# First half of a conv attention kernel: partitions (y half, x), Sx by column tiles without masks, Yh in quarter-array tiles over two banks

## The reference

```python
qkv = einsum('bcxy,oc->boxy', img, w_qkv)            # q, k, v of 512 channels each
k = softmax(k over the 4096 pixels)
content_out = einsum('nde,ndm->nem', einsum('ndm,nem->nde', k, v), q)
Sx = einsum('ndxy,xid->nixy', q4, Px)                # Px[x,i] = rel_rows[i-x+63]
Yh = einsum('nixy,neiy->nexy', Sx, v4)               # then batch norm over all n, x, y
Sy = einsum('ndxy,yid->nixy', q4, Py)                # Py from rel_columns, the same way
rel_pos_out = einsum('nixy,nexi->nexy', Sy, Yh)
out = einsum('bcxy,oc->boxy', content_out + rel_pos_out, w_out) + b_out
```

## Time and profile before

| | |
|---|---|
| median of three runs | 3277.91 us |
| the profiled execution's own time | 3290.07 us |
| its span, first to last instruction | 3288.2 us |
| mean granted TensorE clock | 0.932 of 2.4 GHz |
| PE busy (matmul) | 2756.5 us, 84% |
| DVE busy | 2293.0 us, 70% |
| ACT busy | 1874.7 us, 57% |
| POOL busy | 1111.6 us, 34% |
| first half | from 0 to about 1982 us |

### The profile page before, as it was taken

How to read it: one execution, slowest core, us unless ns; L and a number is a source line. 1 busy time by engine, 2 the same in 40 slices (tenths; PEclk the granted TensorE clock), 3 DMA queues, 4 the chain that set the end, 5 groups by cost and what they waited for, 6 DMA issues and landing times. The chain is left out here.

```text
span 3288.2 us, 102882 instructions
## 1 busy us (share of the span) xinstructions
PE 2756.5 (84%) x42610; PEld 2189.8 (67%) x42610; DVE 2293.0 (70%) x3437; ACT 1874.7 (57%) x3268; POOL 1111.6 (34%) x495
## 2 busy tenths in 40 slices
PE   2898998998997988988989981787978787888888
PEld 2687787776876877777778771656565655665655
DVE  5687787786786876787786665756575656665665
ACT  2575665756666666575575652546464545555553
POOL 1223313224133133142241316553434334352530
PEclk9999999999999999999999995898989898989989
DMA  3133323323324224234232336766766757676663
GB/s 131 44 88 112 87 65 118 92 60 118 86 66 131 67 71 139 60 77 127 66 92 56 79 92 130 149 183 145 185 145 172 159 167 171 161 170 160 160 162 105
DMA packets 419610, 381.99 MB, mean 116 GB/s; under 512 B 296784, under 2 KB 363600, under 8 KB 413008
## 3 DMA queue, kind: packets, MB, share of 16 engines
q1 hardware_dynamic: 399632, 341.13, 41.9%
q10 hardware_dynamic: 19520, 34.15, 2.9%
HBM read 206.37 MB, written 168.82 MB: 114 GB/s over the span
## 5 line engine op out<-in xcount | busy, mean ns | idle before, releaser
L365 PE MATMUL bank<-w_hi,x_hi 128*128 128x256 f16 x2048 | 577.9, 282 | 46.6 <-POOL x_lo L700 23.4
L365 PE MATMUL bank<-w_lo,x_hi 128*128 128x256 f16 x2048 | 570.7, 279 | 0.0
L365 PE MATMUL bank<-w_hi,x_lo 128*128 128x256 f16 x2048 | 570.3, 278 | 0.0
L715 POOL TENSOR_TENSOR k_f<-k_f,negmax 128x1024 f32<-128x1024 f32 x64 | 181.6, 2859 | 940.7 <-DVE negmax L675 940.7
L1153 POOL TENSOR_TENSOR y_f<-y_f,y_mul 128x1024 f32<-128x1024 f32 x126 | 264.6, 2100 | 662.9 <-DMA y_f<-y_scratch 661.6
L1096 DVE TENSOR_TENSOR yb_lo<-y_f,yb_hi 64x1024 f16<-64x1024 f32 x256 | 381.7, 1491 | 80.8 <-ACT yb_hi L996 79.1
L652 DVE SCALAR_TENSOR_TENSOR sx_lo<-bank,parity,sx_hi 128x512 f16<-128x512 f32 x512 | 355.2, 743 | 51.7 <-ACT sx_hi L490 51.1
L942 PE MATMUL bank<-q,rc_both 128*64 128x64 f16 x4096 | 282.9, 245 | 97.9 <-issue 47.0
L480 ACT ACTIVATE k_f<-bank 128x256 f32<-128x256 f32 x512 | 198.8, 388 | 244.2 <-PE bank L365 233.8
L490 ACT ACTIVATE sx_hi<-bank,parity 128x512 f16<-128x512 f32 x512 | 321.2, 703 | 26.1 <-PE bank L365 18.4
L942 PEld LDWEIGHTS bank<-q,rc_both 128*64 128x64 f16 x4096 | 252.4, 134 | 125.0 <-issue 76.4
(11 more groups left out here) (149 smaller groups left out, 9009.0 us busy)
## 6 DMA issues: line engine op xcount, KB each, us to landing
y_scratch<-yst SPq DMA_DIRECT2D x512, 128.0 KB, 2.0
y_f<-y_scratch SPq DMA_DIRECT2D x64, 1024.0 KB, 11.9
q<-q_scratch SPq DMA_DIRECT2D x256, 256.0 KB, 11.9
x_f<-x SPq DMA_DIRECT2D x16, 2048.0 KB, 10.9
q_scratch<-q_hi SPq DMA_DIRECT2D x64, 512.0 KB, 5.8
q_scratch<-q_lo SPq DMA_DIRECT2D x64, 512.0 KB, 7.4
x_res<-x SPq DMA_DIRECT2D x128, 256.0 KB, 4.3
out<-x_res ACTq DMA_DIRECT2D x128, 256.0 KB, 3.3
```

The source lines that it names most:

```text
L365: mm = pe.matmul(outs, lhs[a], rhs[m], start=first and n == 0, stop=last and n == 2, **kw)
L715: pool.tensor_tensor(kk, kk, negmax[:, :].unsqueeze(1).to_broadcast([P, 8, P]), ALU.add).then_inc(shifted_b, 1)
```

## The change

- Partitions: `x_hi`/`x_lo` are kept as (y half, x, y) instead of (x, y half, y). The kv weights then give v and k with partitions (g, x) instead of (x, g); the bytes read per matmul and their strides stay.
- sx: the table holds the two halves one after the other (`g*P`), and each step issues 48 matmuls of 64 weights x 64 columns, two column tiles (g = 0, 1) side by side, instead of 24 of 128 weights. The output partitions are (g, i), the order of v's, so Sx is kept once, without masks: one ACT copy and one DVE subtraction for a step.
- yh: for each y, a tile of 64 rows x 64 weights for each (g, head), 64 columns; g = 0 goes to one bank and g = 1 to the next, so two steps are made together: 96 matmuls for two steps (48 a step instead of 24). PE waits until both banks are free. Both `filled` counts come with the last matmuls of the 96.
- Order in stretch A: q 0, q 1, yh 0, yh 1, q 2, q 3, yh 2, yh 3, ... The chain's pieces stay at the same counts j.
- A yh step holds 8 values of y of one half, and its store is one DMA of twice the size.

```diff
-                if not (first and hp == 0):
-                    order.append(("yh", hp - 1, i))
+                if i % 2 == 1 and not (first and hp == 0):
+                    order += [("yh", hp - 1, i - 1), ("yh", hp - 1, i)]
...
-                    dve.tensor_copy(rr_f[s, g:2 * NREL:2], rel_in[s, 0, :]).then_inc(s_zero, 1)
+                    dve.tensor_copy(rr_f[s, g * P:g * P + NREL], rel_in[s, 0, :]).then_inc(s_zero, 1)
...
-            x_hi = sb("x_hi", [P, CC, PIX], F16, p1)
+            x_hi = sb("x_hi", [P, CC, 2, H, HALF], F16, p1)
...
-                    for g in range(2):
-                        sp.dma_start(y_dram[b * HP + hp, g, 4 * i:4 * i + 4].rearrange("y h e x -> (h e) y x"),
-                                     yst[:, i % YST, :, g, :]).then_inc(y_st[i % YST], 16)
+                    k, g = i // 2, i % 2
+                    sp.dma_start(y_dram[b * HP + hp, g, 8 * k:8 * k + 8].rearrange("y h e x -> (h e) y x"),
+                                 yst[:, i % YST, :, :]).then_inc(y_st[i % YST], 16)
...
                             for j in range(8):
                                 xx = 8 * i + j
-                                mm = pairs(bank[:, r, j * 64:j * 64 + 64],
-                                           [s[:, 2 * (H - 1 - xx):2 * (H - 1 - xx) + P] for s in (rr_hi, rr_lo)],
-                                           [s[:, :, xx // XB, :, xx % XB] for s in (q_hi, q_lo)], True, True)
-                        else:
+                                for k, (a, m) in enumerate(TERMS):
+                                    for g in range(2):
+                                        mm = pe.matmul(bank[g * 64:g * 64 + 64, r, j * 64:j * 64 + 64],
+                                                       (rr_hi, rr_lo)[a][:, g * P + H - 1 - xx:g * P + H - 1 - xx + 64],
+                                                       (q_hi, q_lo)[m][:, :, xx // XB, :, xx % XB],
+                                                       start=k == 0, stop=k == 2)
+                        elif i % 2 == 0:
...
-                            for j in range(4):
+
+                            pe.wait_ge(freed, N + 2)
+                            pe.sem_inc(yh_begun, 1)
+                            banks = (r, (r + 1) % BANKS)
+                            for j in range(8):
                                 y2 = 4 * i + j
                                 for k, (a, m) in enumerate(TERMS):
-                                    for h2 in range(2):
-                                        own = slice(h2 * 64, h2 * 64 + 64)
-                                        mm = pe.matmul(bank[own, r, j * 128:j * 128 + 128],
-                                                       (v_hi, v_lo)[a][:, hp % 2, y2, own],
-                                                       (sx_hi, sx_lo)[m][:, h2 * HALF + y2, :, :].rearrange("p g x -> p (g x)"),
-                                                       start=k == 0, stop=k == 2)
-                        mm.then_inc(filled, 1)
+                                    for g in range(2):
+                                        half = slice(g * 64, g * 64 + 64)
+                                        for h2 in range(2):
+                                            own = slice(h2 * 64, h2 * 64 + 64)
+                                            mm = pe.matmul(bank[own, banks[g], j * 64:j * 64 + 64],
+                                                           (v_hi, v_lo)[a][half, hp % 2, y2, own],
+                                                           (sx_hi, sx_lo)[m][half, h2 * HALF + y2, :],
+                                                           start=k == 0, stop=k == 2)
+                                        if j == 7 and k == 2 and g == 0:
+                                            mm.then_inc(filled, 1)
+                        if kind != "yh" or i % 2 == 0:
+                            mm.then_inc(filled, 1)
...
-                            for g in range(2):
-                                o = act.activation(sx_hi[:, :, g, 8 * i:8 * i + 8],
-                                                   src.rearrange("p (x h) -> p h x", x=8),
-                                                   ACT.Copy, scale=parity[:, g:g + 1])
-                            o.then_inc(hi_done, 1)
+                            act.activation(sx_hi[:, :, 8 * i:8 * i + 8], src.rearrange("p (x h) -> p h x", x=8),
+                                           ACT.Copy).then_inc(hi_done, 1)
...
-                                o = dve.scalar_tensor_tensor(sx_lo[:, :, g, s],
-                                                             src.rearrange("p (x h) -> p h x", x=8),
-                                                             parity[:, g:g + 1], sx_hi[:, :, g, s],
-                                                             ALU.mult, ALU.subtract)
-                            o.then_inc(freed, 1)
+                            dve.tensor_tensor(sx_lo[:, :, s], src.rearrange("p (x h) -> p h x", x=8), sx_hi[:, :, s],
+                                              ALU.subtract).then_inc(freed, 1)
```

More of the change, by code:

```diff
@@ L222, in attention_kernel @@
         with p1, nc.Block() as block:
[L223 to L224 removed]
+            x_hi = sb("x_hi", [P, CC, 2, H, HALF], F16, p1)
+            x_lo = sb("x_lo", [P, CC, 2, H, HALF], F16, p1)
             k_f = sb("k_f", [P, HALF, P], F32, p1)
@@ L232, in attention_kernel @@
             q_lo = sb("q_lo", [P, 2, H // XB, HALF, XB], F16, p1)
-            sx_hi = sb("sx_hi", [P, 2 * HALF, 2, H], F16, p1)
-            sx_lo = sb("sx_lo", [P, 2 * HALF, 2, H], F16, p1)
-            yst = sb("yst", [P, YST, 4, 2, H], F32, p1)
+            sx_hi = sb("sx_hi", [P, 2 * HALF, H], F16, p1)
+            sx_lo = sb("sx_lo", [P, 2 * HALF, H], F16, p1)
+            yst = sb("yst", [P, YST, 8, H], F32, p1)
             k_max = sb("k_max", [P, 8, P], F32, p1)
@@ L278, in attention_kernel @@
             y_stats = sem("y_stats", p1)
+            yh_begun = sem("yh_begun", p1)
             init = sem("init", p1)
@@ L282, in attention_kernel @@
             XC = PIX // NXC
+            XR = H // NXC
             NBN = 16 + 1 + 2 + 2 + 1 + 4 + 2
@@ L295, in chain, with x_piece @@
                 return [(h, j) for h, j in start if 0 <= j < 16]
+            def x_piece(c, j):
+                return x_f[:, c, j * XC:j * XC + XC].rearrange("p (x g y) -> p g x y", g=2, y=HALF)
             def turns(eng, turn):
@@ L302, in turns @@
                 turn(NB - 1, final_turn)
-            xh_kv = [t[:, :, :].rearrange("p c (k y) -> p c y k", y=HALF) for t in (x_hi, x_lo)]
-            xh_q = [t[:, :, :].rearrange("p c (x g y) -> p c g x y", g=2, y=HALF) for t in (x_hi, x_lo)]
+            xh_kv = [t[:, :, :, :, :].rearrange("p c g x y -> p c y (g x)") for t in (x_hi, x_lo)]
             w_kv = [t[:, :, HID:3 * HID].rearrange("p c (t n) -> p c t n", t=2) for t in (w_hi, w_lo)]
@@ L356, in _ @@
                 for s in range(YST):
-                    sp.wait_ge(y_st[s], 32 * (NT * YH // YST + 1))
+                    sp.wait_ge(y_st[s], 16 * (NT * YH // YST + 1))
                 sp.wait_ge(x_in, 16 * CC * NB)
@@ L458, in split_x @@
                     act.wait_ge(x_norm, nth * 8 + piece * CC + 1)
-                    s = slice(piece * XC, piece * XC + XC)
-                    act.activation(x_hi[:, 0, s], x_f[:, 0, s], ACT.Copy).then_inc(x_hi_a, 1)
+                    act.activation(x_hi[:, 0, :, piece * XR:piece * XR + XR, :], x_piece(0, piece),
+                                   ACT.Copy).then_inc(x_hi_a, 1)
                 for piece in range(NXC):
@@ L475, in turn @@
                         if kind == "yh":
-                            act.wait_ge(y_st[i % YST], (t * (YH // YST) + (i // YST + 1)) * 32)
+                            act.wait_ge(y_st[i % YST], (t * (YH // YST) + (i // YST + 1)) * 16)
                         act.wait_ge(filled, at(b, (kind, hp, i)) + 1)
@@ L593, in split_x @@
                 def split_x(nth, j):
-                    s = slice(j * XC, j * XC + XC)
+                    s = slice(j * XR, j * XR + XR)
                     dve.wait_ge(x_norm, nth * 8 + (CC * j + 2))
-                    dve.tensor_copy(x_hi[:, 1, s], x_f[:, 1, s]).then_inc(x_hi_b, 1)
+                    dve.tensor_copy(x_hi[:, 1, :, s, :], x_piece(1, j)).then_inc(x_hi_b, 1)
                     dve.wait_ge(x_hi_a, nth * NXC + (j + 1))
-                    dve.tensor_tensor(x_lo[:, 0, s], x_f[:, 0, s], x_hi[:, 0, s], ALU.subtract).then_inc(x_lo_done, 1)
+                    dve.tensor_tensor(x_lo[:, 0, :, s, :], x_piece(0, j), x_hi[:, 0, :, s, :],
+                                      ALU.subtract).then_inc(x_lo_done, 1)
                 for k in range(16):
@@ L649, in turn @@
                         elif kind == "sx":
-                            for g in range(2):
-                                s = slice(8 * i, 8 * i + 8)
-                                o = dve.scalar_tensor_tensor(sx_lo[:, :, g, s],
```

(12 more changed lines are left out.)

6 lines of the change are left out of this document (3 added, 3 removed).

## The result

The changed kernel took 3306.32 us (median of 9 runs, 3292.87 to 3312.53), the kernel before 3285.02 us (9 runs beside them). The ratio is 1.0053, with a 95% interval from 1.0031 to 1.0075: slower by half a per cent. The sign was right, the size was not: the time lies between the forecast and the faster rival (3212 us, chance 0.14), and well nearer to no change than to either.

A forecast was written before the change was run, and what follows sets the result against it. PE was taken to bound nearly everything. B +134 us, A 31 x 0.6, last head pairs -10, first -2, very last -2.5 gave +138: 3428 us from 3290.07, or 3416 as median; range 3355 to 3510.

The forecast's parts named there:

- The sign: Whole kernel: slower, chance 0.83; within 0.2% 0.03; faster 0.14.
- faster rival: sx on PE: short matmuls in tiles overlap fully, 30 ns a pair, -66 us, 3212 us; chance 0.14.
- sx on PE: Each sx step: 24 pairs of column tiles at Sy's 62 ns, 1.49 us a step, where 0.72 us before.
- B: Stretch of sx and kv in turn, 23 head pairs: 23.8 us, against 17.2, 17.7 and 19.2 before; cost 134 us.
- B and C of the last head pairs: Last head pair of an image, sx alone then kv: 14.5 us against 14.9, then 21.0 against 22.7.
- changes of tiling: PE switching between 128x128 and column tiles: 0.1 us, twice for each sx among kv.
- lower bound: sx pair on PE: 30 ns, 0.72 us a step, if a strided moving operand in tiles were no slower than the present sx.
- yh on PE: yh steps in stretch A: 12 groups of four quarter tiles a step, 0.72 us taken, where 0.67 us before.
- first rival: yh on PE: quarter tiles don't overlap beyond pairs, 31 ns a matmul, 1.49 us a step, 3500 us; chance 0.21.
- Stretch A by hand: Stretch of q and yh: 28.0 us against 27.4, +0.6, with PE waits of 2.8 and 1.1 us.
- Half clock: Stretch B: half speed costs 1.7 us before; after, sx is blind to it, so 1.3 us.
- DVE and ACT relief: sx pieces: about 0.65 us a step saved on each, some 170 us busy time each, worth something only in last head pairs' B.

The follow-up runs named there:

- sy_contig: Changed kernel with Sy in the second half reading q as 64 neighbouring elements instead of 32 pieces of two (wrong q values): ratio 0.9961 to the kernel before.
- late_phi: Changed kernel with the four copies to p_hi on ACT two steps later and p_lo on POOL one step later: ratio 0.9955 to the kernel before.
- yh_pairs: Changed kernel with yh one bank at a time, two quarter tiles side by side, order q, yh, q, yh: ratio 1.0051 to the kernel before.
- sx_whole: Changed kernel with sx as 24 full-array matmuls instead of 48 on column tiles, half of Sx wrong: ratio 0.9867 to the kernel before.
- sx_twos: Changed kernel with two sx steps in a row, then two kv steps, where they alternate: ratio 1.0024 to the kernel before.
- fill_after: Changed kernel with unread matmuls in PE's idle time, 20 ahead of yh 6 and 10 ahead of sx 0: ratio 0.9986 to the kernel before.

## Why the prediction was wrong, by its own steps

**sx on PE, "I take 24 x 62 = 1.49 us a step": this step failed.** It measured 0.77 us plus 0.03. I priced the pair by the row of the same weights, columns and tiles (Sy), and called the moving operand a reason only in the rival. sy_contig shows that the moving operand makes all of the difference. The inference behind it held for Sy (a rate that is the same at both clocks is not set by the columns) but did not carry over: the new sx does follow the clock (54 ns a pair at half clock, 33 at full), and so does Sy with the other operand. By the step: the period of sx and kv on PE is 2.36 us (0.77 + 0.13 + 1.26 + 0.20) where I had 3.0, so 0.64 x 8 x 23 = 118 us too much, against the 120 us by which the profiled execution missed the sum. That the two agree so well is luck. B itself is 19.9, 20.1 and 19.8 us where I had 23.8, 89 us less in all, because a longer half clock and waits took up the rest; A came out 44 us below its forecast in all, and B and C of the last head pairs 15 us above theirs.

The sign is in part luck too. The term that was to make the kernel slower, 0.77 us more for a step's pairs, was 0.08. What did make B longer are the changes of tiling, which the forecast had as a small term and rightly sized, and the half clock, which it let shrink.

The lower bound I gave, 30 ns by the present sx, was the row with the same moving operand, and it was nearly right. Its rival then failed at the other end: at a pair of 33 ns it said faster, because it set its sum of steps for B, 17.6 us, against the measured 17.2, and so had B "where it was" although it counted 0.2 us of changes in each step, and took the half clock for 1.3 us. B is 2.2 us longer by the steps alone (7 x 0.30 + 0.08): 0.19 us of changes, 0.08 of pace, 0.03 in the kv behind. So its turning point, 36 ns, was too high; nor does it follow from the rival's own sums, where -66 us at 30 ns and 4.4 us for each ns of the pair (24 x 8 x 23 pairs) give 45 ns.

The sum had a slip besides: the 0.6 us of A stand in the 31 head pairs and again in the seven last head pairs of an image, 4 us too much.

The Trainium skill's rule on weight loads below 128 columns (TensorE: Matmul & The Clock Gate, Weight-path perf modes and LDWEIGHTS), 53 ns for 64 columns, does not hold as the pace of a pair here: sx runs at 33 ns and Sy, with its operand changed, at 32 ns.

**yh on PE, 0.72 us a step:** 0.39. Quarter tiles overlap by four and the first rival (31 ns a matmul) is out.

The measured 8 ns a matmul also rule out the 25 ns a matmul that I had worked out, as an estimate, from the overhead of 60 cycles that the Trainium skill states (TensorEngine Tiling, Instruction Overhead).

**Stretch A by hand, 28.0 us:** 26.8. The waits were forecast as 2.8 and 1.1 us and came as 2.87 and 1.27. I put the 1.2 us down to the yh steps ahead of the softmax chain, four steps at 0.3 us less each; no run shows it. The step's reason, that the chain on ACT sets the end, was right (late_phi, yh_pairs): PE time saved ahead of the two waits became waiting.

**Half clock, "after, sx is blind to it, so 1.3":** too small, and a second step that failed. The longer wait ahead of yh 6 was followed by 6.4 us at half clock in a head pair instead of 2.6, and sx is not blind to it. Of the whole, filling the idle time gave back 0.7% (1.0053 to 0.9986).

**DVE and ACT relief:** 0.686 us on DVE and 0.600 on ACT for a step, as taken, and in B worth what was said: B of last head pairs 14.3 us on the mean (forecast 14.5; 14.8 before). C of these did not shrink (22.9 against 22.5; forecast 21.0).

The sum by what was measured, in us: B of the 23 head pairs where sx and kv alternate +0.95 x 7, +3.1 x 8 and +2.4 x 8, their A -0.7 x 23, their C +0.1 x 23, A, B and C of the seven last head pairs of an image -1.3 x 7 together: +28. All up to the end of the very first head pair -4, the very last head pair +3 (B 14.6 instead of 10.9, with one of the waits "issue", 4.2 us, in it), the eight yh behind it -6, the way to the first Sy -1: +20, as measured.

## What to carry to other kernels

Price a matmul that isn't in the trace by the row with the same moving operand as well as the same tiles, and if two rows disagree by two, look for what differs between them before choosing. Time saved on an engine just ahead of a wait that another chain sets turns into idle time, and here it brought a longer stretch at half clock with it; look at which wait ends last after the change, and at the clock behind it. Alternating tile shapes at a fine grain cost about 0.2 us a turn here and can eat a change whose matmuls are nearly as fast as before. Relief of engines that nobody waits for pays little: of 139 and 168 us off DVE and ACT, all that shows is half a microsecond in the B of seven head pairs. A kernel with the reference's Sx from the full array, in the change's partition order, was not run; sx_whole's 0.9867 suggests what it could give.

## What the runs showed of the hardware

- Two column tiles with 64 weights and 64 columns each take 33 ns together at full clock, 54 at half, and four quarter tiles 33 ns together: PE took a weight load and a matmul every 8 ns, for 96 in a row.
- A moving operand in 4-byte pieces 128 bytes apart doubles the time of 64-column pairs at full clock, from 32 to 62 ns (sy_contig); 2-byte elements 4 bytes apart don't (sx, 33 ns).
- From a full-array matmul to column tiles and back costs 0.09 and 0.10 us beyond the distance within either (changed kernel, stretch B).
- PE waits for nothing that the profile shows ahead of sx in column tiles: 14 us in the first half of the changed kernel, 29 and 30 us in sx_twos, late_phi and fill_after, none ahead of sx with half the instructions.
- Unread matmuls in idle time keep the granted clock at 1.0 (285 to 90 us at half clock in the first half of the changed kernel, 195 to 101 in the kernel before), and gave 0.6% to the kernel before.
